# Cross-attention and mixture of experts on one core: VectorE takes over a copy of the gate weights, ScalarE's other copy and one set of row statistics move to later slots

## The reference

```python
x = x + xattn(layernorm(x), ctx)      # scores normalised by the mean and variance of each batch, softmax, values, Wo
h = layernorm(x)
shared = swiglu(h @ sw1 + sb1) @ sw2 + sb2
probs = softmax(h @ gate_w + gate_b)
cw = probs where it is one of the two largest of the 8, else 0      # the gate weights, [tokens, 8]
routed = sum over the experts e of cw[:, e] * (swiglu(h @ rw1[e] + rb1[e]) @ rw2[e] + rb2[e])
x = x + shared + routed
```

## Time and profile before

| what | value |
|---|---|
| time, median of 3 runs | 133.92 us (133.74 to 134.27) |
| the profiled execution's own time | 133.8 us |
| its span in the trace | 132.0 us |
| granted TensorE clock | 0.999 |
| TensorE busy | 126.3 us, 96% |
| VectorE busy | 101.4 us, 77% |
| ScalarE busy | 87.3 us, 66% |
| GpSimd busy | 48.3 us, 37% |

### The profile page before, as it was taken

How to read it: one execution, slowest core, us unless ns; L and a number is a source line. 1 busy time by engine, 2 the same in 40 slices (tenths; PEclk the granted TensorE clock), 3 DMA queues, 4 the chain that set the end, 5 groups by cost and what they waited for, 6 DMA issues and landing times.

```text
span 132.0 us, 2199 instructions
## 1 busy us (share of the span) xinstructions
PE 126.3 (96%) x639; PEld 98.5 (75%) x639; DVE 101.4 (77%) x303; ACT 87.3 (66%) x172; POOL 48.3 (37%) x75
## 2 busy tenths in 40 slices
PE   7999999889999999999999999999999999999992
PEld 7777797658586786688688786798678778777871
DVE  1398688696997999759747999459797877889862
ACT  1547978999365269976695269975672997647250
POOL 7174254056961420458635420453244075000000
PEclk9999999999999999999999999999999999999999
DMA  3999400001730000079000002079000106910022
GB/s 94 315 353 263 149 5 2 0 0 40 320 129 0 0 0 2 5 235 386 22 0 0 0 0 79 5 232 377 37 0 0 67 17 194 369 72 0 5 79 79
DMA packets 8829, 12.98 MB, mean 98 GB/s; under 512 B 1321, under 2 KB 6994, under 8 KB 8306
## 3 DMA queue, kind: packets, MB, share of 16 engines
q1 hardware_dynamic: 8242, 12.62, 27.7%
q10 hardware_dynamic: 576, 0.23, 0.7%
HBM read 11.73 MB, written 1.11 MB: 97 GB/s over the span
## 4 chain that ended last, share of the span: by engine, by line
PE 69%; DVE 17%; issue 6%; ACT 3%; POOL 2%; DVEq 0%; ACTq 0%; POOLq 0%
PE bank L1031 61%; DVE silu L914 2%; PE bank L1095 2%; PE bank L1146 2%; ACT prob L547 2%; DVE sim_stats L773 1%; DVE act L922 1%; PE bank L1047 1%; POOL sim_r L435 1%; POOL ln_rstd L429 1%; PE bank L1123 1%; DVE g_beats L865 1%; DVE g_rank L868 1%; ACT x_head L586 1%; DVE g_diff L862 1%
## 5 line engine op out<-in xcount | busy, mean ns | idle before, releaser
L466 POOL TENSOR_TENSOR act_rest<-act,act_head 128x256 fp32r<-128x256 f32 x32 | 22.8, 736 | 35.6 <-ACT act_head L597 23.2
L1031 PE MATMUL bank<-x_head,w_head 128*128 128x512 f32 x72 | 31.5, 437 | 0.3 <-issue 0.3
L630 ACT ACTIVATE bank<-bank,b_cols 128x512 f32<-128x512 f32 x25 | 16.5, 659 | 18.4 <-PE bank L1031 18.1
L1031 PE MATMUL bank<-x_head,w_rest 128*128 128x512 f32 x72 | 28.5, 396 | 0.0
L1031 PE MATMUL bank<-x_rest,w_head 128*128 128x512 f32 x72 | 28.5, 395 | 0.0
L922 DVE SCALAR_TENSOR_TENSOR act<-bank,b_cols,silu 128x512 f32<-128x512 f32 (+1 forms) x34 | 24.9, 734 | 3.6 <-ACT silu L630 2.5
L914 DVE TENSOR_TENSOR silu<-bank,cw_all 128x512 f32<-128x512 f32 x25 | 17.2, 686 | 3.2 <-ACT bank L630 2.5
L1031 PEld LDWEIGHTS bank<-x_head,w_head 128*128 128x128 f32 x72 | 13.6, 189 | 4.4 <-issue 1.5
L1031 PEld LDWEIGHTS bank<-x_head,w_rest 128*128 128x128 f32 x72 | 13.5, 188 | 3.3
L1031 PEld LDWEIGHTS bank<-x_rest,w_head 128*128 128x128 f32 x72 | 13.6, 189 | 2.6 <-issue 0.5
L597 ACT CAST act_head<-act 128x512 fp32r<-128x512 f32 x22 | 13.5, 615 | 1.1 <-DVE act L922 0.6
(11 more groups left out here) (133 smaller groups left out, 232.3 us busy)
## 6 DMA issues: line engine op xcount, KB each, us to landing
cw_all<-cw_dram SPq DMA_DIRECT2D x4, 1024.0 KB, 7.0
cw_all<-cw_dram SPq DMA_DIRECT2D x4, 512.0 KB, 5.0
cw_all<-cw_dram SPq DMA_DIRECT2D x6, 256.0 KB, 3.5
x_sb<-in_x_dram SPq DMA_DIRECT2D x4, 256.0 KB, 4.1
w_sb<-in_L_ffn_rw_dram SPq DMA_DIRECT2D x1, 1024.0 KB, 7.2
ctx_sb<-in_ctx_dram SPq DMA_DIRECT2D x4, 192.0 KB, 4.0
out_dram<-x SPq DMA_DIRECT2D x3, 256.0 KB, 2.1
w_sb<-in_L_ffn_rw_dram SPq DMA_DIRECT2D x1, 512.0 KB, 6.4
```

The lines of the kernel that those rows point to most:

```text
L466: pool.tensor_tensor(act_rest[:, m % 3, cols], act[:, m % 4, cols], act_head[:, m % 3, cols].bitcast(F32), ALU.subtract).then_inc(pool_res ...
L630: scalar.activation(silu_out, hid(n, 0)[:, cols], ACT.Silu, bias=b1_cols[:, 0, e:e + 1]).then_inc(silu_sb, 1)
L1031: return pe.matmul(dst, lhs, rhs, start=start, stop=stop, skip_group_check=True)
```

## The change

`cw_copy` is divided into three. `cw_row_copy(c)`, the 8x512 copy to `cw_rows`, goes to VectorE at slot 9, place 1: step 9c - 2, between scaled(n) and act(n). `heads_with_weights(c)` stays where `cw_copy` stood. `cw_parts_copy(c)`, the 48x512 copy to `cw_t`, goes to the next step's place 1 on ScalarE, behind its SiLU. `first_statistics(3)` goes from step 8, place 0, to step 9, place 2. Chunk 0 has its own `first_cw_copy`, with the same two copies on ScalarE.

```diff
-        ACT_AT = {..., 'router_exp': [9, 1], 'cw_copy': [10, 1]}
-        DVE_AT = {'first_statistics': [-8, 0], ..., 'router_weights': [9, 0]}
+        ACT_AT = {..., 'router_exp': [9, 1], 'heads_with_weights': [10, 1], 'cw_parts_copy': [11, 1]}
+        DVE_AT = {'first_statistics': [-7, 2], ..., 'router_weights': [9, 0], 'cw_row_copy': [9, 1]}
...
-            def cw_copy(c):
+            def first_cw_copy():
+                scalar.wait_ge(cwt_ps, 1)
+                scalar.wait_ge(consts_ready, 3 + E)
+                copy(cw_t[HEAD_ROWS:ROWS_END, :], LATE[HEAD_ROWS:ROWS_END, :]).then_inc(cwt_sb, 1)
+                copy(cw_rows[:, 0, :], LATE[0:E, :]).then_inc(cwrow_sb, 1)
+
+            def heads_with_weights(c):
+                if NX * c - 2 in WITH_WEIGHTS:
+                    act_heads(NX * c - 2)
+
+            def cw_parts_copy(c):
                 scalar.wait_ge(cwt_ps, c + 1)
-                if c >= 2:
-                    scalar.wait_ge(cw_out, 16 * (c - 1))
-                if c == 0:
-                    scalar.wait_ge(consts_ready, 3 + E)
-                    copy(cw_t[HEAD_ROWS:ROWS_END, :], LATE[HEAD_ROWS:ROWS_END, :]).then_inc(cwt_sb, 1)
-                copy(cw_rows[:, c % 2, :], LATE[0:E, :]).then_inc(cwrow_sb, 1)
-                if c >= 1:
-                    if NX * c - 2 in WITH_WEIGHTS:
-                        act_heads(NX * c - 2)
-                    scalar.wait_ge(y_ps, NX * (c - 1) + 2)
-                    scalar.wait_ge(cw_ps, BY_PRODUCT)
-                    copy(cw_t[HEAD_ROWS:ROWS_END, :], LATE[HEAD_ROWS:ROWS_END, :]).then_inc(cwt_sb, 1)
+                scalar.wait_ge(cwrow_sb, c + 1)
+                scalar.wait_ge(y_ps, NX * (c - 1) + 2)
+                scalar.wait_ge(cw_ps, BY_PRODUCT)
+                copy(cw_t[HEAD_ROWS:ROWS_END, :], LATE[HEAD_ROWS:ROWS_END, :]).then_inc(cwt_sb, 1)
...
+            def cw_row_copy(c):
+                dve.wait_ge(cwt_ps, c + 1)
+                if c >= 2:
+                    dve.wait_ge(cw_out, 16 * (c - 1))
+                dve.tensor_copy(cw_rows[:, c % 2, :], LATE[0:E, :]).then_inc(cwrow_sb, 1)
```

More of the change, by code:

```diff
@@ L272, in xattn_moe_kernel @@
         PE_AT = {'transpose_inputs': [-4, 1], 'project_u': [-4, 2], 'project_v': [-4, 2], 'scores': [-3, 1], 'scores_average': [-1, 4], 'attend': [3, 4], 'transpose_x2': [6, 4], 'router': [7, 4], 'transpose_cw': [10, 4], 'transpose_prob': [1, 4]}
-        ACT_AT = {'input_copies': [-4, 1], 'u_copies': [-4, 1], 'v_copies': [-4, 1], 'exponentials': [0, 2], 'normalise': [5, 1], 'prob_copies': [2, 2], 'x2_heads': [7, 0], 'router_exp': [9, 1], 'cw_copy': [10, 1]}
-        DVE_AT = {'first_statistics': [-8, 0], 'statistics_0': [-4, 2], 'x2_rests': [7, 0], 'statistics_1': [-2, 0], 'variance': [-1, 1], 'scale': [-1, 2], 'residual': [3, 2], 'second_shift': [4, 2], 'router_logits': [8, 0], 'router_select': [8, 2], 'router_weights': [9, 0]}
+        ACT_AT = {'input_copies': [-4, 1], 'u_copies': [-4, 1], 'v_copies': [-4, 1], 'exponentials': [0, 2], 'normalise': [5, 1], 'prob_copies': [2, 2], 'x2_heads': [7, 0], 'router_exp': [9, 1], 'heads_with_weights': [10, 1], 'cw_parts_copy': [11, 1]}
+        DVE_AT = {'first_statistics': [-7, 2], 'statistics_0': [-4, 2], 'x2_rests': [7, 0], 'statistics_1': [-2, 0], 'variance': [-1, 1], 'scale': [-1, 2], 'residual': [3, 2], 'second_shift': [4, 2], 'router_logits': [8, 0], 'router_select': [8, 2], 'router_weights': [9, 0], 'cw_row_copy': [9, 1]}
         POOL_AT = {'first_rstd': [-7, 1], 'scores_rstd': [-1, 1], 'second_rstd': [4, 0]}
@@ L280, in xattn_moe_kernel @@
                    ("router_weights", 0), ("first_statistics", 2), ("project_v", 2), ("v_copies", 2),
-                   ("transpose_cw", 0), ("cw_copy", 0), ("attend", 1)}
+                   ("transpose_cw", 0), ("heads_with_weights", 0), ("cw_parts_copy", 0), ("cw_row_copy", 0), ("attend", 1)}
         EARLIER = 2
@@ L681, in _ @@
             expert_silu(0, 1)
-            cw_copy(0)
+            first_cw_copy()
             prob_copy(2)
@@ L697, in _ @@
                       "prob_copies": prob_copies, "x2_heads": lambda c: x2_heads(c, 0),
-                      "normalise": lambda c: normalise(c, 0), "router_exp": router_exp, "cw_copy": cw_copy}
+                      "normalise": lambda c: normalise(c, 0), "router_exp": router_exp, "heads_with_weights": heads_with_weights, "cw_parts_copy": cw_parts_copy}
             for n in range(NX * C):
@@ L1001, in _ @@
                       "second_shift": lambda c: second_shift(c, 0), "x2_rests": lambda c: x2_rests(c, 0),
-                      "router_logits": router_logits, "router_select": router_select, "router_weights": router_weights}
+                      "router_logits": router_logits, "router_select": router_select, "router_weights": router_weights, "cw_row_copy": cw_row_copy}
             def run(n, place):
```

## The result

| | before | changed |
|---|---|---|
| median, 7 runs each | 133.92 us (133.74 to 134.27) | 134.89 us (134.53 to 135.03) |
| ratio | | 1.0055, 95% interval 1.0033 to 1.0077 |
| a second measurement | 133.87 us | 134.76 us, ratio 1.0067 (1.0042 to 1.0093) |
| span of the profiled execution | 132.0 us | 133.1 us |
| TensorE's granted clock | 0.999 | 1.0 |

What follows compares the result with a forecast made beforehand. TensorE was taken as the bound, its chain unbroken at chunk 3. Terms -0.12, +0.12 and +0.99 made +1.0 us on 133.8, 134.8; with half the median's 0.12 offset, forecast 134.9 us, range 134.2 to 135.6.

Steps and rivals of the forecast that it cites:

- The sum: Whole kernel: -0.12, +0.12 and +0.99 make +1.0 us on the profiled execution's 133.8, which is 134.8.
- What bounds the kernel: TensorE, busy 96%, makes the chain from 82.78 us on; any wait put before its instructions there adds in full.
- The term of chunk 3, +0.99: Step 27's second half: transposes, copy, act(25), matmul in a loop; second matmul at 108.35 against 107.36, +0.99 us.
- The price of the copy: VectorE's 8x512 copy from PSUM taken as 0.60 us, between bounds of 0.33 and 0.72.
- The quick copy: Rival: copy takes 0.33 us, chunks 1 and 2 don't stall, chunk 3 loses 0.72; +0.5, 134.3 us; chance 0.10.
- Chunk 2, +0.12: TensorE's second matmul behind act(16) at 83.68 against 83.56, +0.12 us; no hole there to swallow it.
- chunk 1, -0.12: Stall of 0.12 at act(7), but ScalarE's earlier head closes the 0.24 hole before step 7's product: net -0.12 us.
- The 48x512 copy and the statistics: Copy behind ScalarE's SiLU is off the path; statistics behind act(9) fit VectorE's idle time: cost zero.
- The bound of 0.1 "if the cover were gone": Statistics in step 9: some 0.1 us if VectorE's idle time no longer covered them.
- SyncE's queue: cw_rows ready 1.7 us earlier in chunk 1, about 1 in chunk 2, unchanged in chunk 3; TensorE's waits unaffected: zero.
- the cascade: Rival: late work behind act(25) stalls TensorE again and releases take 0.12 us; +1.8, 135.6 us; chance 0.12.
- the faster outcome: Rival: holes of chunks 1 and 2 close and chunk 3's stall doesn't come; -0.7, 133.1 us; chance 0.05.

Runs made afterwards that it cites:

- e12: The changed kernel measured once more, with no further edit: 134.76 us, ratio 1.0067 to the kernel before.
- e5: Changed kernel with the 8x512 copy on VectorE for chunk 3 alone, on ScalarE for chunks 1 and 2: 134.74 us, ratio 1.0065 to before.
- e3: Changed kernel with the 8x512 copy back on ScalarE, but VectorE still waiting for the transposes before act(n): 134.44 us, ratio 1.0036 to before.
- e4: Changed kernel with a second 8x512 copy on VectorE, into a spare tile, behind the first: 136.76 us, ratio 1.0210 to before.
- e6: Changed kernel with the 8x512 copy on VectorE for chunks 1 and 2, on ScalarE for chunk 3: 133.89 us, ratio 0.9993 to before.
- e1: Changed kernel with VectorE's 8x512 copy behind act(n) instead of in front of it: 133.75 us, ratio 0.9988 to before.
- e2: Changed kernel with the 8x512 copy back on ScalarE in front of the head: 133.97 us, ratio 1.0005 to before.
- e8: Changed kernel with the last chunk's statistics back in step 8, in front of scaled(8): 136.13 us, ratio 1.0170 to before.
- e9: e8 with GpSimd's rest of step 7 also waiting until VectorE has written ln_veps: 135.38 us, ratio 1.0112 to before.
- e10: Changed kernel with the 8x512 copy behind act(n) and the statistics back in front of scaled(8): 134.87 us, ratio 1.0073 to before.
- e11: e1 measured once more, the changed kernel with the 8x512 copy behind act(n): 133.63 us, ratio 0.9985 to before.

## Why the prediction was right

- **The number.** The sum was +0.99 on the profiled execution's 133.8, which rounds to 134.8; the profiled execution took 134.92, and the marks of the table show +0.99 and +1.01. This agreement is earned by the terms below. That the median of 134.89 lies within 0.01 us of 134.9 is luck: medians of this kernel move by 0.1 to 0.2 us, and the ratio of this measurement alone would put the loss at 0.7 us.
- **What bounds the kernel.** Right. From 82.78 us to its last microseconds the chain was TensorE's alone, and the wait put into it came out in full: +0.99 at one matmul, +0.98 in W3-O, so what stands behind it gave nothing back.
- **The term of chunk 3, +0.99.** Measured +0.98 in the changed kernel, +0.98 in e12, +0.98 in e5 where it stands alone. Its parts: release 0.04 (taken 0.05), copy 0.60 (0.60), act 0.73 (0.75), release 0.06 (0.05), restart 0.34 (0.32, from a pair of matmuls behind transposes, not behind a stall). e3 separates wait from copy, 0.39 and 0.59; e4 adds one more copy and 0.60.
- **The price of the copy.** No VectorE copy stood in the trace of before; the choice of 0.60 between 0.33 and 0.72 rested on the one-input operations from PSUM. The row is 0.68 long, the next operation starts 0.60 or 0.61 later. What the queue pays is this distance from start to start. The quick copy of 0.33 us is out by it. The Trainium skill, "VectorE: DVE Perf Modes", section on the TRN2 errata, has 120 cycles plus one per column, by my estimate 0.66 us; that is near the row's length (0.68) and 0.06 above what the queue pays. The Trainium skill, same page, section on why PSUM operands drop a tier, allows no doubled rate for float32 from PSUM, and the row agrees.
- **Chunk 2, +0.12, and chunk 1, -0.12.** Measured +0.11 and -0.11. e6 shows both without chunk 3. In chunk 1 the head came earlier on ScalarE (2.43 us behind the start of the transposes, 2.90 before), GpSimd's rest with it, and the hole of 0.24 closed; e1, without the stall, shows the gain alone, -0.23, and e2, with the copy in front of the head again, shows none. The trace of before names no releaser for this hole. That the rest ended it and not the head is read from the times: the head was over at 54.59, the rest at 56.11, and the product's first matmul started at 56.25.
- **The 48x512 copy and the statistics: nothing.** Right by e2 and by the changed kernel, where the statistics fit into VectorE's idle time in step 9 and 0.40 us of it is left. The bound of 0.1 "if the cover were gone" spoke of this new place, and no run tested it. What the prediction did not ask is what the old place would cost once the copy is in the queue: 0.99 us (e8), of which e9 puts down 0.52 to the statistics' length and 0.47 to the meeting with GpSimd. So this part of the change is worth nothing alone and 0.99 us beside the copy. The prediction had the first half only.
- **SyncE's queue: nothing.** Right for the changed kernel, where TensorE is late enough in chunk 3. In e1, e6, e10 and e11 the return of the weights does cost time, see below.
- **The rivals.** The quick copy is ruled out by the row; the cascade did not come, since the chain stays on TensorE from 108.18 to its last microseconds; the faster outcome would have needed act(25) by 107.0 and it ended at 108.12. e1 shows that the faster side was there, one place further down in the same table.

## What to carry to other kernels

Before an operation that waits for another engine is put into a queue, ask what stands behind it and whether the engine waited for wants exactly that: here transposes, copy, act and matmul closed a loop of 1.77 us where 0.78 us of TensorE's work was there to cover it, and one place later the same copy was free. Look at each place that a table entry stands for: two of three chunks had the cover, the third did not, and it made the whole loss. Where the engine behind it never waits otherwise, the price of a VectorE operation is its start-to-start distance (0.60 us for 512 PSUM columns), not its row's length (0.68).

## What the runs showed that was not expected

**A small VectorE operation beside GpSimd.** ln_veps reads and writes SBUF. Beside GpSimd's L466 it took 0.62 us (e8) and 0.73 us (e10) in place of 0.17, and with GpSimd held back 0.17 (e9). In both traces it ended 0.02 us behind the end of the first of the two GpSimd operations (which stand as one row, x2), so it was held for the rest of that operation. This is not so for every pair. In the timeline of e8 ln_veps itself takes 0.17 us beside another GpSimd operation, and a reciprocal of the same size takes 0.17 beside L466:

```profile
7.45 3.26 POOL L420 TENSOR_TENSOR row_powers<-ln_veps,powers 128x8 f32<-128x8 f32 x2 [3.69 <-DVE ln_veps L757]
8.59 0.17 DVE L757 TENSOR_SCALAR ln_veps<-ln_mv 128x4 f32<-128x4 f32 x1
```

```profile
88.03 2.81 POOL L466 TENSOR_TENSOR act_rest<-act,act_head 128x256 fp32r<-128x256 f32 x4 [1.39 <-ACT act_head L597]
90.08 0.17 DVE L824 RECIPROCAL row_inv<-row_sum 128x4 f32<-128x4 f32 x1
```

The scaled products and the acts, which read one operand from PSUM, ran at their usual 0.68 to 0.75 us beside GpSimd rows too. What sets the held pair apart no run shows. The Trainium skill, "GPSIMD Engine Reference", section on specifications, says that GpSimd's SBUF interfaces are shared with VectorE and that there is contention with VectorE instructions in a two-port mode or with two SBUF inputs. Whether ln_veps ran in such a mode no row tells; that it was held in e8 and e10 would agree, that it was not held beside L420 would not.

**A second bound right behind the first.** Chunk 3's weights go to memory and back, and chunk 3's first gated product waits for them. ScalarE's output copy is queued behind it, and TensorE's down product of step 27 waits for that copy. From the timeline of the kernel before:

```profile
112.01 0.69 DVE L903 TENSOR_TENSOR act<-bank,cw_all 128x512 f32<-128x512 f32 x1 [0.34 <-DMA cw_all<-cw_dram]
...
114.00 0.19 PEld L1031 LDWEIGHTS bank<-act_head,w_head 128*128 128x128 f32 x1 [0.15 <-ACT out_t L638]
```

And from that of e11, the copy behind act for the second time:

```profile
112.22 0.69 DVE L911 TENSOR_TENSOR act<-bank,cw_all 128x512 f32<-128x512 f32 x1 [0.77 <-DMA cw_all<-cw_dram]
...
114.20 0.19 PEld L1039 LDWEIGHTS bank<-act_head,w_head 128*128 128x128 f32 x1 [0.45 <-ACT out_t L640]
```

The idle time in the second row and the last stretch of the table go together: 0.15 and 17.49 (before), 0.17 and 17.48 (e2), 0.23 and 17.53 (e1), 0.32 and 17.63 (e6), 0.32 and 17.64 (e10), 0.45 and 17.78 (e11). Up to 0.17 us of idle time before the weight load costs nothing that the stretch shows; what is above comes on top. Two things make it up. With the copy behind act on VectorE (e1, e10, e11) cw_rows is ready 1.43 to 1.44 us behind the start of the transposes, on ScalarE (before, e2, e6) 1.28 to 1.30. And from there to the gated product it takes 4.67 to 4.91 us, which differs between executions of the same kernel (4.67 in e1, 4.90 in e11). So of the 0.23 us gained in chunk 1 a part is given back at step 27, in e1 0.04, in e11 all of it; in the changed kernel the stall of 0.98 us hid it. Whether a faster round trip in chunk 3 would turn e1 into a gain that the times show was not tried.
